# Scores and transpositions of an attention kernel on TensorE: two heads of each in turn, in place of one

## What is computed

```
qkv = x @ W_w.T + W_b                         # 16 heads of 8 features
attn = einsum('bhqd,bhkd->bhqk', q, k) / sqrt(128)
attn = where(causal, -inf, attn) + bias       # a relative bias per head
w = softmax(attn, axis=-1)
o = einsum('bhqk,bhkd->bhqd', w, v)
y = x + o @ proj_w.T + proj_b                 # then a layer norm
```

## Time and profile before

| what | us |
|---|---|
| median of 3 runs | 728.5 |
| lowest and highest run | 728.35, 734.0 |
| the profiled execution | 729.18 |
| its span in the profile | 726.7 |
| PE busy in the span | 624.5 |
| DVE, ACT and POOL busy | 448.8, 373.2, 468.9 |

### The profile page before, as it was taken

The page is one execution under the profiler, slowest core; times in us unless marked ns, Lnnn a source line. Parts: engine busy times, 40 slices in busy tenths (PEclk is TensorE's granted clock), DMA queues, the critical chain, the costliest instruction groups (busy, mean ns, idle before and its releaser), DMA issues. The chain is left out here.

```text
span 726.7 us, 15498 instructions
## 1 busy us (share of the span) xinstructions
PE 624.5 (86%) x4794; PEld 518.4 (71%) x4794; DVE 448.8 (62%) x1825; ACT 373.2 (51%) x904; POOL 468.9 (65%) x591
## 2 busy tenths in 40 slices
PE   5797899999999999999995399699994999999820
PEld 3595677777777776689994287587993999999620
DVE  6537988888888788554442746446771333333696
ACT  6634677777777777634442554123553433333331
POOL 7534578988989889455554744275775466666444
PEclk9668999999999999999998559799997999999965
DMA  8552535454444445157774300421112578773534
GB/s 256 165 163 102 181 132 156 152 179 133 139 150 155 154 162 189 58 181 234 234 236 140 86 1 1 154 94 41 55 50 85 154 236 246 230 244 100 142 115 116
DMA packets 85888, 105.42 MB, mean 145 GB/s; under 512 B 9584, under 2 KB 66160, under 8 KB 85808
## 3 DMA queue, kind: packets, MB, share of 16 engines
q1 hardware_dynamic: 75168, 77.84, 36.1%
q0 software_dynamic: 7616, 17.32, 6.9%
q10 hardware_dynamic: 3024, 9.29, 3.4%
HBM read 69.43 MB, written 34.98 MB: 144 GB/s over the span
## 5 line engine op out<-in xcount | busy, mean ns | idle before, releaser
L1442 POOL DMA_INDIRECT tok<-h_y_out,h_x_in x78 | 74.6, 957 | 47.0 <-DVE h_y_out L1748 34.8
L922 DVE CUSTOM_DVE_ANT_0 a_high<-a_p_s,f_shared 128x256 f32<-128x256 f32 x168 | 70.1, 417 | 33.4 <-PE a_p_s L588 32.4
L1435 POOL DMA_INDIRECT slots<-k_xn,k_pos x64 | 63.8, 997 | 39.2 <-issue 13.7
L1741 DVE TENSOR_TENSOR h_hid<-h_k,h_pre 128x512 f32<-128x512 f32 x39 | 27.0, 691 | 82.4 <-ACT h_pre L1653 82.4
L831 ACT ACTIVATE a_prob_more<-a_p_t 128x384 f32<-128x384 f32 x128 | 61.8, 498 | 30.7 <-PE a_p_t L602 30.5
L1196 POOL TENSOR_TENSOR a_high<-a_high,a_top 128x768 f32<-128x768 f32 x42 | 61.6, 1467 | 24.6 <-DVE a_top L922 23.6
L587 PE MATMUL a_p_s<-a_kst,a_qst 72*128 72x256 bf16 x256 | 73.3, 288 | 3.1 <-DVE a_top L922 2.2
L1525 PE MATMUL h_k<-h_x_t,h_w 128*128 128x256 f32 x312 | 74.8, 383 | 0.0
L1242 POOL DMA_INDIRECT tok<-a_fill,a_e_ids x46 | 44.3, 963 | 43.3 <-DVE a_fill L1128 34.2
L1525 PEld LDWEIGHTS h_k<-h_x_t,h_w 128*128 128x128 f32 x312 | 57.1, 193 | 6.3
L588 PE MATMUL a_p_s<-a_kst,a_qst 72*128 72x128 bf16 x256 | 57.8, 226 | 0.0
(11 more groups left out here) (273 smaller groups left out, 1863.7 us busy)
## 6 DMA issues: line engine op xcount, KB each, us to landing
h_w<-in_W SPq DMA_DIRECT2D x39, 384.0 KB, 3.2
a_e_w<-in_W SPq DMA_DIRECT2D x23, 514.0 KB
a_kst<-parts SPq DMA_DIRECT2D x32, 288.0 KB
a_qst<-parts SPq DMA_DIRECT2D x32, 288.0 KB
slots<-a_fill ACTq DMA_DIRECT2D x21, 432.0 KB, 6.2
parts<-a_part SPq DMA_DIRECT2D x32, 192.0 KB
h_x_in<-slots SPq DMA_DIRECT2D x39, 144.0 KB, 3.2
h_top<-tok SPq DMA_DIRECT2D x16, 256.0 KB, 3.5
```

The costliest lines, as they stand in the source:

```text
L922: dve.tensor_tensor_reduce(out=out[:, x, :], in0=p_s[n % banks][:, cols], in1=bias_q[:, h, at], scale=1.0, scalar=-3.0e38, op0=ALU.add, op ...
L1435: pool.indirect_dma_start(D["slots1"], bass.IndirectOffsetOnAxis(ap=R.pos[n][:, t:t + 1], axis=0), R.xn[:, t, :], None).then_inc(done, 16)
L1442: pool.indirect_dma_start(D["tok1"], bass.IndirectOffsetOnAxis(ap=x_in[r][:, k, P:P + 1].bitcast(I32), axis=0), y_out[r][:, k, :], None).t ...
```

## The change

In a quad, PE issues the scores of heads 0 and 1, then the transpositions of heads 0 and 1, then the scores of heads 2 and 3, then the transpositions of heads 2 and 3. No instruction is added or removed, and the streams of the other engines are as before. `rank` in quad 4 now follows the transposition of head 1.

```
             for n in range(last):
                 b, g = divmod(n, quads)
-                for x in range(QUAD):
-                    if n + 2 < last:
-                        score(pe, n + 2, x)
-                    turn(pe, n, x)
+                for x in range(0, QUAD, 2):
+                    for y in (x, x + 1):
+                        if n + 2 < last:
+                            score(pe, n + 2, y)
+                    for y in (x, x + 1):
+                        turn(pe, n, y)
                     if n == RANKED and x == 0:
                         rank(pe)
```

## The result

The changed kernel took 738.04 us (median of 4 runs), against 730.51 us for the kernel before in the same comparison: a ratio of 1.0117, with a 95% interval from 1.007 to 1.0164. A second comparison in more rounds gave 1.0116 (1.0082 to 1.0150). The changed order is slower by a little over 1%. The span of the profiled execution went from 726.7 to 734.2 us.

What follows compares the result with a forecast made beforehand. Bound by the chain from turn 0 through ACT's numerators to turn 3: 7.0 us for 13 batches plus 0.1 for the last, 0 at half clock, on 728.5 gives 735.6 us (ratio 1.0097), range 730.5 to 740.0.

Steps and rivals of the forecast that it cites:

- The costs on PE: PE's matmul spacings in a quad: score after score 0.05, transposition after transposition 0.11, so turn 0 0.16 us later, turn 1 0.06 earlier.
- The rival of the bare weight load: On PE, score after score costs 0.15 in place of 0.05, 5.2 us more, 740.8 us; chance 0.14.
- The chain turn 0, numerator 0, work between, numerator 1, turn 3: PE to ACT and back: late turn 0 delays turn 3 by 0.16 us in g = 1 to 3, 0.06 in g = 0.
- Nothing behind turn 3 takes it back: PE's work behind turn 3 shifts with it, as do DVE and POOL, so a batch grows by the full 0.54 us.
- 13 batches x 0.54 = 7.0 us: Steady loop, quads 8 to 59: each of 13 batches is 0.54 us longer, 7.0 us in all.
- The stage at half clock: 0: Quads 0 to 7, much of the time at half clock: no net cost, between -0.9 and +0.6 us.
- The shift reaches the end whole: Experts and second layer follow the loop's end unchanged, so the loop's delay adds fully to the time: 7.0 + 0.1 us.
- Waits behind turn 3 take it up: Idle 0.41 ahead of g = 1 and g = 3 absorbs delays of g = 0 and g = 2: 4.2 us, 732.7 us; chance 0.19.

Runs made afterwards that it cites:

- the first 12 quads alone: Changed order in quads 0 to 11 only, the old order behind, against the kernel before: 729.26 us, ratio 0.9993.
- the first-pair-old kernel: Kernel before with only the second pair changed (score 0, turn 0, score 1, turn 1, score 2, score 3, turn 2, turn 3): 732.83 us, ratio 1.0042.
- the two faster loops: Kernel before with each turn of the first pair ahead of its score in g = 2 and 3: 0.9988; the same with ACT's copies behind numerator 1: 0.9982.
- both edits together: Kernel before with turn 0 first in g = 2 and 3 and ACT's copy_o, read_v, copy_ot behind numerator 1: 727.98 us, ratio 0.9982.

## Why the prediction was right

The forecast was 735.6 us with a ratio of 1.0097; the measured ratio is 1.0117 in one comparison and 1.0116 in the other, and 738 us lies inside the range of 730.5 to 740.0. The chance of slower by over 1% was put at 0.41 and that of no change at 0.56, so the side that the prediction favoured was missed by 0.2%, which is less than the intervals (from 1.007 and from 1.0082) can tell.

- *The costs on PE.* Score after score 0.05, transposition after transposition 0.11, turn 0 at 0.29, turn 1 at 0.57: all as forecast. The rival of the bare weight load is out. The rule of the Trainium skill (TensorE: Matmul & The Clock Gate, Part 3, The mechanism), by which a load on the same rows would not overlap, does not hold here: it overlapped for scores (0.05) as for transpositions (0.11). Only score 3 came later than forecast, at 1.19 in place of 1.12, and nothing waited for it.
- *The chain turn 0, numerator 0, work between, numerator 1, turn 3.* Forecast 0.16 in g = 1, 2 and 3, and 0.06 in g = 0; measured 0.17, 0.16, 0.16 and 0.05. Putting the first pair back removed all of it, taking `copy_ot` out of the chain removed it in g = 3, and turn 0 earlier moved turn 3 earlier. This is shown.
- *"Nothing behind turn 3 takes it back."* This step failed, by 0.09 us in g = 1 of each batch: `turn_o` had been waiting for DVE's `affine`, whose time hangs on the first score of g = 0. The prediction said the latter of DVE's run, but did not see that a delay within g = 1 then meets a time that stays. A batch grew by 0.44 (16.08 in ten of the thirteen batches, against 15.64 or 15.65) in place of 0.54. The wait could be seen in the kernel before (0.29 ahead of `turn_o`, where other places show 0.20).
- *13 batches x 0.54 = 7.0 us.* Measured 5.3 us from quad 12 to 60, which is twelve batches, and 5.8 for all thirteen. A size was off, in the term above: 0.44 in place of 0.54.
- *The stage at half clock: 0.* The timed runs of the first 12 quads alone agree (0.9993, from 2.1 us less to 1.1 more), the 0.4 us of quads 8 to 11 included.
- *"The shift reaches the end whole."* Not settled. By the medians the changed kernel is 7.5 and 8.3 us slower where its loop explains 5.8; the first-pair-old kernel is 2.7 us slower with a loop that explains nothing; the two faster loops win 0.6 and 1.4 us where the profile shows 2.4 and 3.5. Beyond their intervals go three of these: the first-pair-old kernel (at least 1.4 us over), both edits together (at most 2.6 us won) and, by 0.2 us, the second comparison of the change. The even comparison of the kernel before with itself rules out a bias of over 0.27%. Changes in the spans of single profiles (up to 5.5 us ahead of quad 12, 4 us behind the loop) are too large for one profile each to show where 2 us lie. The cause stays open. That the forecast came so near the ratio rests in part on luck: the steady cost was forecast too high (7.0 for 5.8), and an excess that it did not have made up for it.
- *"Waits behind turn 3 take it up", 0.19.* It named the idle times ahead of g = 1 and g = 3. These kept their 0.41, so it was wrong where it stood; the wait that did take something up stood elsewhere.

## What to carry to other kernels

When two engines pass work to and fro, look at which instruction starts the other engine's chain in each round: a score of 0.16 us placed ahead of it made the last turn 0.16 us later in three quads of four, while with the first pair in its old order the same move behind it lengthened no quad. Ask of each copy on the other engine whether it stands inside that chain. Before counting a delay as passed on whole, look at each instruction behind it for an idle time longer than its like has elsewhere.

## What the runs showed that was not expected

**An instruction queue's packet beside the first loads of the experts.** Behind the loop PE waits for the first tile of the experts' tokens (L663). In the kernel before it started after an idle time of 0.41 us; in the changed one:

```profile
308.75 0.20 PEld L663 LDWEIGHTS a_p_qk<-k_ident,a_fill 128*128 128x128 f32 x2 [1.63 <-DMA a_fill<-slots]
```

The second profile of the kernel before shows 1.97 at the same place, so it isn't the change:

```profile
303.11 0.20 PEld L663 LDWEIGHTS a_p_qk<-k_ident,a_fill 128*128 128x128 f32 x2 [1.97 <-DMA a_fill<-slots]
```

The DMA views of the six us from the start of quad 63, of the kernel before in its first profile and then in its second:

```profile
a_fill<-slots SPq DMA_DIRECT2D x4, 144.0 KB, 2.3
```

```profile
q8 instruction: 1, 0.02, 0.9%
a_fill<-slots SPq DMA_DIRECT2D x3, 144.0 KB, 3.9
```

Of 14 profiles, nine had such a packet of an instruction queue in that stretch and a median landing of 3.3 to 3.9 us. Four had none, and 2.3 us. One had the packet and 2.3 us. So the two mostly go together; that the packet is the cause, and what decides when it falls, wasn't tried. The longer wait is 1 to 2 us of the differences behind the loop from one execution to the next. The profile of the first-pair-old kernel had neither the packet nor the longer wait, and its start of quad 12 was 2.8 us late, so in that execution the excess lay elsewhere.

**The clock ahead of the steady part.** The granted clock changes several times ahead of quad 12, at other times in each execution. In the first profile of the kernel before and in its second, from 84 to 88 us (the last three numbers are the clock, the DMA share and GB/s):

```profile
84.00:88.00 4.00, 4.00 (x56) 2.78 (x49) 4.00 (x26) 2.67 (x7) 2.58 (x5) 1.00 0.33 130
```

```profile
84.00:88.00 4.00, 4.00 (x48) 2.73 (x40) 2.94 (x21) 2.24 (x6) 1.44 (x5) 0.79 0.09 34
```

PE fell to 1.2 GHz for a part of this stretch in one execution of the same kernel and not in the other. In the changed kernel quad 8 fell into such a stretch (0.74) and took 3.96 us in place of 3.09. This is why one profile's start of quad 12 (97.8 to 103.4 us over all runs) says little of a change, while the 186 us behind it repeat to 0.1 us.
